# A gated state-space block ahead of six attention layers: a third state row on GpSimd, and D x written to the output bank by ScalarE

## What is computed

```python
xr, gate = split(x @ W_in.T);  xr = xr + t_emb
xc = silu(conv over 4 steps(xr));  xn = layernorm(xc) * ln_g + ln_b      # 256 channels
Bm, Cm, dt = split(xn @ W_xproj.T, 3)                                    # 16 states each
dt = tanh(dt @ W_dt.T + b_dt) * 0.01;  Ad = 1 + dt * (-tanh(A_log));  Bd = Bm * min(norm(xn), 1)
for each of the 32 steps:                                                # h: 16 rows x 256 channels
    h = clip(h * Ad + Bd x xn, -10, 10)
    y = sum over the 16 rows of Cm * h
out = ((y + D * xn) * silu(gate)) @ W_out.T
```

## Time and profile before

| | us |
|---|---|
| runs of the kernel before, median of 3 | 2906.71 (2904.49 to 2908.19) |
| the profiled execution, its own time | 2910.12 |
| its span in the trace | 2908.3 |
| first stage of `cond_block` | 0 to about 93 |
| recurrence, to the start of `stack` | about 93 to 397.3 |
| `stack` and `add_input` | 397.3 to 2908.3 |
| busy share of the span, PE / DVE / ACT / POOL | 94% / 91% / 78% / 73% |

### The profile page before, as it was taken

How to read it: one execution, slowest core, us unless ns; L and a number is a source line. 1 busy time by engine, 2 the same in 40 slices (tenths; PEclk the granted TensorE clock), 3 DMA queues, 4 the chain that set the end, 5 groups by cost and what they waited for, 6 DMA issues and landing times. The chain is left out here.

```text
span 2908.3 us, 91012 instructions
## 1 busy us (share of the span) xinstructions
PE 2731.2 (94%) x35457; PEld 2099.1 (72%) x35457; DVE 2634.1 (91%) x3407; ACT 2266.7 (78%) x3792; POOL 2137.5 (73%) x1529
## 2 busy tenths in 40 slices
PE   8799978999999999999999999999999999999985
PEld 7688866777777777777777777777777777777763
DVE  7899968999999999999999999999999999999972
ACT  5688857878787887878787887878787888878771
POOL 6777758777778777787777787777877777777750
PEclk9899999999999999999999999999999999999996
DMA  1000012232223232232322232322322322322222
GB/s 54 22 1 1 1 37 71 69 74 68 70 63 76 68 75 70 64 75 69 74 67 64 69 77 72 75 63 65 77 71 61 76 66 67 71 61 62 65 58 62
DMA packets 103838, 178.36 MB, mean 61 GB/s; under 512 B 29222, under 2 KB 52836, under 8 KB 103524
## 3 DMA queue, kind: packets, MB, share of 16 engines
q1 hardware_dynamic: 102500, 174.69, 24.7%
q10 hardware_dynamic: 1152, 1.20, 0.1%
HBM read 22.72 MB, written 2.10 MB: 9 GB/s over the span
## 5 line engine op out<-in xcount | busy, mean ns | idle before, releaser
L1395 POOL TENSOR_TENSOR spare<-spare,qk_t 128x1024 f32<-128x1024 f32 x384 | 910.8, 2394 | 10.9 <-POOL xs_lo L1381 8.1
L811 PE MATMUL pa<-w_hi,xs_hi 128*128 128x512 f32 x1152 | 511.5, 444 | 27.7 <-issue 8.4
L1411 POOL TENSOR_TENSOR sm<-sm,inv 128x512 f32<-128x512 f32 x192 | 202.1, 1052 | 448.3 <-DVE sm L1267 385.0
L1236 DVE TENSOR_TENSOR spare<-pa,rot 128x1024 f32<-128x1024 f32 x384 | 464.0, 1208 | 0.0
L1245 DVE TENSOR_TENSOR qk_t<-pa,rot 128x1024 f32<-128x1024 f32 x384 | 463.8, 1208 | 0.0
L1229 DVE TENSOR_REDUCE ss<-spare 128x16 f32<-128x1024 f32 x384 | 457.0, 1190 | 6.7 <-ACT spare L992 5.9
L811 PE MATMUL pa<-w_hi,xs_lo 128*128 128x512 f32 x1152 | 456.6, 396 | 0.5 <-DMA pT<-prT 0.5
L811 PE MATMUL pa<-w_lo,xs_hi 128*128 128x512 f32 x1152 | 454.8, 395 | 0.0
L840 PE MATMUL px<-ident_sb,spare 128*128 128x128 f32 x3072 | 407.6, 276 | 23.0 <-POOL spare L1404 11.4
L1404 POOL TENSOR_TENSOR spare<-spare,inv 128x1024 f32<-128x1024 f32 x192 | 366.2, 1907 | 78.5 <-ACT inv L1031 73.8
L840 PEld LDWEIGHTS px<-ident_sb,spare 128*128 128x128 f32 x3072 | 340.1, 141 | 113.1 <-issue 61.3
(11 more groups left out here) (160 smaller groups left out, 6065.8 us busy)
## 6 DMA issues: line engine op xcount, KB each, us to landing
kT<-spare SPq DMA_DIRECT2D x384, 256.0 KB, 3.7
pT<-prT SPq DMA_DIRECT2D x768, 64.0 KB, 2.0
w_part<-in_Wqkv SPq DMA_DIRECT2D x40, 192.0 KB, 3.7
wo<-in_Wo SPq DMA_DIRECT2D x6, 512.0 KB, 5.5
c_h<-in_x SPq DMA_DIRECT2D x4, 512.0 KB, 9.1
o_x<-in_x SPq DMA_DIRECT2D x8, 256.0 KB, 4.8
out<-o_out SPq DMA_DIRECT2D x8, 256.0 KB, 4.2
wo<-in_W SPq DMA_DIRECT2D x6, 341.0 KB, 4.6
```

The source lines that it names most:

```text
L811: last = pe.matmul(pa[(u + c) % 2][:, half * 512:half * 512 + 512], x[:, j * P:(j + 1) * P], w[:, at], start=(k == 0), stop=(k == 2))
L1236: dve.tensor_tensor(heads(qk_r[:, c, :]), heads(pa[(3 * j + c) % 2][:]), per_head(rot[:, l % 2, 2 * c, :]), ALU.mult).then_inc(s[cos], 1)
L1395: pool.tensor_tensor(qk_r[:, c, :], qk_r[:, c, :], qk_t[:, c, :], ALU.add)\
L1411: pool.tensor_tensor(keys(sm[:]), keys(sm[:]), over(inv[:, j % 2, 0, :], S), ALU.mult)\
```

## The change

The constant PS goes from 2 to 3. So GpSimd does rows 0, 1 and 2 in its two `side` instructions, which have 128x768 elements instead of 128x512, ScalarE makes three products for SBUF, and 13 rows are left for the PSUM banks and VectorE. They still make 7 pairs, the last of which has one row. And D x: TensorE's product with the identity goes, and ScalarE copies the row of `dx` into the PSUM bank ahead of the 16 products, all of which then add to what stands there. The copy of step t+1 stands in ScalarE's list between the second pair of step t+1 and `copy_xnT`, and has the waits that the product had, `z_ready` among them, and a new semaphore, `skip_written`, for TensorE.

```diff
-PS = 2
+PS = 3
...
                 def y_product(t):
                     if t < S:
-                        pe.wait_ge(s["dx_ready"], t + 1)
-                        wait_for(pe, s["z_ready"], t - 1)
-                        if t < 2:
-                            pe.wait_ge(s["pre_ready"], S)
-                        pe.matmul(py[t % 2][:, 0:DI], ident[:], dx[:, t, :], start=True, stop=False)
+                        pe.wait_ge(s["skip_written"], t + 1)
                         pe.wait_ge(s["cdiag_ready"], t + 1)
                         pe.wait_ge(s["h_ready"], t + 1)
                         for n in range(DS):
                             last = pe.matmul(py[t % 2][:, 0:DI], cdiag[:, t % 3, n, :], h[:, t % 2, n, :], start=False,
-                                             stop=(n == DS - 1))
+                                             stop=(n == DS - 1), skip_group_check=True)
                         last.then_inc(s["y_done"], 1)
...
+                def write_skip(t):
+
+                    if t < S:
+                        act.wait_ge(s["dx_ready"], t + 1)
+                        wait_for(act, s["z_ready"], t - 1)
+                        if t < 2:
+                            act.wait_ge(s["pre_ready"], S)
+                        act.copy(py[t % 2][:, 0:DI], dx[:, t, :]).then_inc(s["skip_written"], 1)
...
                 outer(0, 0, 2)
+                write_skip(0)
                 for t in range(S + 3):
                     outer(t, 2, 3)
                     tanh_dt(t + 1)
                     outer(t, 3, NPAIR)
                     side_outer(t + 1)
                     outer(t + 1, 0, 2)
+                    write_skip(t + 1)
                     copy_xnT(t + 3)
                     write_res(t - 3)
                     copy_zT(t - 2)
```

More of the change, by code:

```diff
@@ L134, in cond_block @@
             xnT_done xnT_ready proj_done bc_ready dt_ready dtt_ready decay_mul decay_ready side_u_ready side_mul side_ready
-            u_ready u_read h_ready cdiag_ready y_done z_ready zT_done zT_ready out_done res_written""".split()
+            skip_written u_ready u_read h_ready cdiag_ready y_done z_ready zT_done zT_ready out_done res_written""".split()
         s = {n: sem("c_" + n) for n in names}
```

## The result

The kernel before takes 2907.45 us (median of 6 runs, 2904.49 to 2909.25), the changed one 2919.09 us (6 runs, 2915.05 to 2926.15). The ratio is 1.0044, with a 95% interval of 1.0030 to 1.0058: slower by 12.8 us by the ratio (the two medians differ by 11.6). The forecast was 2924, slower by 17.4, with a range of 2917 to 2936.

What follows compares the result with a forecast made beforehand. VectorE's list was taken to bound the kernel at 8.94 us a step, afterwards GpSimd's list plus one clip. Median 2906.7, +18.5 (29 steps), +2.0 (first steps), -3.1 (last step) gave 2924.1 us; range 2917 to 2936.

Steps and rivals of the forecast that it cites:

- (b): Order in a step: VectorE's clip gets in before GpSimd's diagonals; 9.60 us a step, +17.4 us, chance 0.5.
- The hold: A clip that meets a running GpSimd instruction waits for its end, then takes about 2.16 us; GpSimd is held likewise.
- The no-hold rival: Clip and diagonals overlap in a running step; VectorE's list is the period, 8.50 us: 2893 or 2905; chance 0.07.
- GpSimd's prices: Side instructions growing from 512 to 768 elements: multiplication 0.43 us more, addition 0.56, together 0.99 us a step.
- The ring in (a): GpSimd's list plus one clip per step: 8.73 us in the old step 2, with 0.99 more 9.72 us.
- (a): Order in a step: clip waits for the diagonals, ends 2.16 us after them; 9.72 us a step, +24.0 us, chance 0.28.
- The delay by the copy: ScalarE's copy for D x waits for the gated product, so the third pair and VectorE come 0.4 us later.
- The ring in (b): GpSimd's list plus one clip, without its 0.13 us wait for the clip: 9.59, say 9.60 us a step.
- The sum: GpSimd's steps 2 to 31 and the ends: (b) +18.5, +2.0, -3.1, together +17.4 us; (a) +22.0, +2.0, together +24.0.
- The first steps: Start of the recurrence: clip of step 0 held, GpSimd's step 2 begins at 119.36 instead of 117.38; +2.0 us.
- close call: In step 2 VectorE is ready for its clip at 122.85, 0.3 us before the diagonals start at 123.18.
- TensorE's clock: Rival: y at half clock behind a pause, 0.4 us over every other step, +6 us, with (a) or (b), chance 0.15.

Runs made afterwards that it cites:

- the run with the added products: The changed kernel with nine products of no use in TensorE's list ahead of the y of step 2; median 2914.12 us of 9 runs, ratio 1.0035.
- the first set: First of three sets of follow-up runs, four of the ten, taken beside 20 runs of the kernel before, median 2908.14 us.
- The forced order: The changed kernel with the diagonals of step t+1 also waiting for the clip of step t; median 2921.91 us of 5 runs, ratio 1.0046.

## Why the prediction was right, and where it was off

The direction, the mechanism and the range held, the range with some luck: a kernel that always keeps (b), with its measured 10.2 to 11.0 us, would be at 2917.7 to 2918.5, just above the lower end of 2917. Point by point:

- **The hold.** Read from three places in the first steps. Shown by the sum in place of the clip: no hold, 1.00 us a step less. The no-hold rival is out.
- **GpSimd's prices.** Forecast 1.47 and 1.83 us for 768 elements, measured 1.467 and 1.814. The multiplication grew by 0.43 us as by the rows' slope, not by the 0.55 that the estimate from the Trainium skill's 2.6 cycles an element (GPSIMD Engine Reference, "Elementwise — side-by-side cycle accounting") gave.
- **The ring in (a).** Forecast 9.72, measured 9.69; the clip's row 3.28 (about 3.2), GpSimd's wait 2.28 (2.3), TensorE's 1.21 (1.2).
- **The delay by the copy.** Forecast 0.4 us, measured 0.33, and hidden in (a) as forecast; by itself it costs 6.8 us of recurrence. In (b) VectorE had 0.70 us to spare before each clip, where I reckoned 0.4.
- **The ring in (b), the term that was mis-sized.** Forecast 9.59 to 9.60, measured 9.36. I took (a)'s ring and struck out only its wait of 0.13. But in (b) the tiny decay instructions lie beside the clip: from the first one's start to the diagonals' start it takes 133.88 - 131.39 = 2.49 us, clip included, where I had counted their 0.48 and then 2.16 for the clip, 2.64. That is 0.15; 0.04 more is the next instruction's start, which in an unbroken list comes 3.57 us after the diagonals' and not 3.61, and 0.03 is what (a) was over as well; 0.02 is left. Over 29 steps the 0.24 make 7.0 us.
- **The sum.** For (b) I forecast +17.4; the two traces that keep (b) show +10.2 and +11.0 at the start of the layers. With the ring's 7.0 taken off, the forecast is +10.4. For (a) I forecast +24.0 and the trace shows +22.2; two of its 29 steps still have 9.36 (0.7 less), and 27 have 9.69 instead of 9.72 (0.8 less). The first steps added 1.4 us and not 2.0, the last step was 0.6 shorter than before, and behind the clip of step 31, where I had nothing change, it took 0.9 longer: the y of step 30 took 8.83 us, and the last y had to wait for it. The measured 12.8 lies between the two courses, near (b).
- **The first steps.** I had the clip of step 0 held, since the diagonals would start at 101.13 and VectorE come at 101.5. It came at 100.83, the diagonals' row starts at 100.86, and it was they that waited (5.73 us). Step 2 of GpSimd began at 118.73 instead of my 119.36. I had the clip of step 1 behind the diagonals; it came ahead of them, and so did that of step 2:

```profile
110.01 2.29 DVE L537 TENSOR_SCALAR c_h<-c_h 128x4096 f32<-128x4096 f32 x1 [0.88 <-POOL c_h L422]
...
112.34 3.60 POOL L440 TENSOR_TENSOR c_cdiag<-c_ident,c_bc 128x2048 f32<-128x2048 f32 x1
...
122.18 2.29 DVE L537 TENSOR_SCALAR c_h<-c_h 128x4096 f32<-128x4096 f32 x1 [3.73 <-POOL c_h L422]
```

So VectorE stood idle for 3.73 us before the clip of step 2, and my "close call" of 0.3 us was none. Order (b) in step 2 was the forecast outcome, but it did not come about by my reckoning.

- **TensorE's clock, the step that failed.** I wrote that a y at half clock costs nothing much, since "VectorE looks for y only a step later", with 8.83 us as the longest one. With y at 10.16 the gated product of the next step was 0.98 late and VectorE 1.38 late at the clip, where (b) had room for 1.00, and (a) stayed for all the steps that follow. What I listed as a rival at 0.4 us for each such step was the switch between my two main cases, worth 12 us. This is read from the rows of the traces; the run with the added products does not test it.

Settled by the runs: the hold, the two parts' own costs, that there are two courses. The traces with y at 10.16 (two kernels) go over to (a), those with 8.83 or 7.07 (three traces) stay in (b). Left open: how often the changed kernel takes either course (by the estimate above one run of six, and the trace taken was that one), and what makes a y 8.83 or 10.16 us long. The spread of its runs, 11.1 us, is about that of the kernel before, 10.5, since the layers vary by 8 us by themselves. That variation goes with TensorE's clock: of the 20 runs before of the first set the six at 2904.4 us or less have a mean granted clock of 0.983 to 0.984, the fourteen at 2906.6 or more one of 0.978 to 0.983. Why the clock differs was not looked for.

## What to carry to other kernels

Idle time of an engine is only room if it can work in it: of GpSimd's 2.50 us of idle time 2.2 lay beside a VectorE instruction that shuts it out, and the new row had to go over the 0.2 that were left. Before moving work to GpSimd, add to its list every VectorE instruction that excludes it, and compare that sum with the period; what looked like 6.4 us in 8.9 was 8.7. And where two lists exclude each other, look at who arrives first in a step: the order can be stable both ways, and a disturbance in the first steps may choose it for the whole loop.

## What was not expected

- A loop with two stable courses, 9.36 and 9.69 us a step, in the same program; which one came went with how long one y took in step 2 (8.83 or 10.16 us).
- An instruction of GpSimd that stood next in its list started 0.05 us behind the clip that had shut it out; one that waited for the clip's semaphore started 0.17 behind it. The forced order had 9.50 us a step, the free one 9.36.
- The time of the unchanged layers varied from 2504.1 to 2512.1 us over 12 traces, more than the whole difference between some of the kernels here.
